# High and low part of each split stationary operand interleaved element by element in one tile

## The chip, the cores and the metric

The kernel runs on one core of a Trainium2 chip. The metric is the device time of one execution in microseconds (us). The core has a matrix engine (TensorE, rows `PE` for its matmuls and `PEld` for its loads of the stationary operand), a vector engine (VectorE, `DVE`), a scalar engine (ScalarE, `ACT`), a general engine (GpSimd, `POOL`) and a synchronising engine (`SP`) from which nearly all transfers are issued. On-chip memory has 128 partitions; a tile of shape 128x512 has 512 elements in each of them.

## What is computed

A Mamba2 layer whose output is gated by a feed-forward network with 4-bit weights, on two sequences of 512 tokens with 512 features. The reference, cut to what matters here:

```
xn   = layernorm(x)                                   # x: [2, 512, 512]
proj = xn @ in_proj_w.T                               # 8192 gate, 8192 x, 1024 B, 1024 C, 128 dt
gate, xBC, dt = split(proj)
xBC  = silu(depthwise_conv4(xBC) + conv_b)
y    = ssd(x, B, C, D, dt)                            # 128 heads of 64, 8 groups, chunks of 128 tokens
yg   = y * silu(gate)
out  = yg * rsqrt(mean(yg**2 over a group) + 1e-5) * norm_w
s    = out @ out_proj_w.T
h    = silu(xn @ W1.T) * (xn @ W3.T)                  # W1, W3: [1376, 512], unpacked from 4 bits
g    = silu(h @ W2.T)                                 # W2: [512, 1376]
return x + s * g
```

## The kernel before, in words

Projections are computed in fp32r, a 32-bit type that TensorE takes in one pass. To keep the precision of float32, each operand `a` is split into a high part `a_hi` (the value as a copy into fp32r leaves it) and a low part `a_lo = a - a_hi`, and each product is three matmuls: hi by hi, hi by lo, lo by hi. `split_mm` (lines 132 to 138) does that for the input projections: its lines 135, 136 and 137 take the stationary operand from `a_hi`, `a_hi` and `a_lo`; `out_mm` (lines 632 to 634) does it for the output projection with `y_hi`, `y_hi`, `y_lo` stationary, and line 832 for the last product of the feed-forward network with `h_hi`, `h_hi`, `h_lo` stationary. Every one of these matmuls has its own load of the stationary operand, 128 (at one place 96) columns out of 128 partitions (96 in the last of the row tiles of `h`). The moving operand has 512 columns, in line 832's last token tile twice 256. The other matmuls of the loop are in full float32, with operands that the change leaves alone, and 128 columns wide: line 544 (`fp32_chunks`), line 586 (`y_diag`), line 694 (transposes of `xt`).

The work is 16 bodies (2 sequences x 8 groups of heads) of 8 steps, each step one tile of 128 channels, software-pipelined by hand: in a step TensorE does `y_off` (L544, 3 chunks in 6 passes), `conv` (12 matmuls of `split_mm` for the tile three steps ahead), `y_diag` (L586 and L544), `gate_mm` (12 of `split_mm`, two ahead), `out_mm` (12, two behind) and `turn_x` (L694); twice in a body `project_bc` adds 12 more. The order on each engine is the order of the code; engines meet at semaphores alone.

Stationary tiles: `conv_hi[i]`, `conv_lo[i]` (lines 185 and 186: three of each, shape [4, 128], for the x, B and C projections), `gate_hi[h]`, `gate_lo[h]` (193, 194: two of each, [4, 512]), `y_hi`, `y_lo` (231, 232: [2, 512]), `up_hi`, `up_lo` (243, 244: four of each, [4, 128]), `h_hi`, `h_lo` (248, 249: [11, 1024]). The high part is written by ScalarE (lines 845, 863, 870, 977, 1135, 1166; the first six gate pieces by GpSimd, line 1495), the low part by GpSimd, which reads the source and the high part (lines 1485, 1490, 1497, 1505, 1528, 1535, 1542, 1585, 1607). In each of them the elements of a partition lie side by side, 4 bytes apart. The moving operands (`xn_hi`, `xn_lo`, `wout_hi`, `wout_lo`, `w2_hi`, `w2_lo`) are split in the same way and stay as they are.

A low part is made well ahead of its use. The semaphores `wlo_x`, `wlo_b`, `wlo_g` and `lo_done` tell TensorE that the low part of conv, B/C, gate and y tiles is there. GpSimd's step runs: `yt + ec` (1519), `yt * gate` (1523), the low parts of the weights (1528, 1535, 1542, 1546), the sum of squares (1555), the low part of y (1505).

Before the loop, tiles of a start phase (`pre`, lines 203 to 221) lie where `wout`, `acc`, `y` and others lie later; the feed-forward tiles (from line 241) lie where the loop's tiles lay.

Of the kernel before, what the change touches and what calls it, by code (L numbers as in the profile page):

```python
# [22 lines left out]
R32 = mybir.dt.float32r  # L23
I32 = mybir.dt.int32

P = 128
SEQS, SEQ, DIM = 2, 512, 512
KT = DIM // P
# [4 lines left out]
HALF = GCH // 2  # L33
# [12 lines left out]
MT = HIDDEN // P  # L46
# [104 lines left out]
def build(nc, x, w_conv, w_gate, w_out, w_dt, conv_p, norm_p, head_p, consts, w1q, w1s, w3q, w3s,  # L151
# [9 lines left out]
    with ExitStack() as ctx:  # L161
# [3 lines left out]
        def alloc(stack, name, shape, dt=F32):  # L165
            return stack.enter_context(nc.sbuf_tensor(name, [P] + shape, dt))
# [8 lines left out]
        dc_all = alloc(ctx, "dc_all", [GROUPS, TILES])  # L175
        cw_all = alloc(ctx, "cw_all", [GROUPS, CONVS, 5])
        alloc(ctx, "to_line", [40])
        ident = alloc(ctx, "ident", [P])
        mask = alloc(ctx, "mask", [P])
        xn_hi = alloc(ctx, "xn_hi", [KT, SEQS * SEQ], R32)  # L180
# [1 line left out]

        main = ExitStack()

        conv_hi = [alloc(main, f"conv_hi{i}", [KT, P], R32) for i in range(3)]
        conv_lo = [alloc(main, f"conv_lo{i}", [KT, P], R32) for i in range(3)]
        raw_x = alloc(main, "raw_x", [2, DIM])
        raw_b = alloc(main, "raw_b", [DIM])
        raw_g = alloc(main, "raw_g", [DIM])
        raw_o = alloc(main, "raw_o", [DIM])  # L190
        z = alloc(main, "z", [3, SEQ])
        b_t = alloc(main, "b_t", [SEQ])
        gate_hi = [alloc(main, f"gate_hi{h}", [KT, HALF], R32) for h in range(2)]
        gate_lo = [alloc(main, f"gate_lo{h}", [KT, HALF], R32) for h in range(2)]
        c_t = alloc(main, "c_t", [2, SEQ])
        xt = alloc(main, "xt", [4, SEQ])
        gm = alloc(main, "gm", [NC, CHUNK])
# [5 lines left out]
        pre = ExitStack()  # L203
# [7 lines left out]
        ecs = alloc(pre, "ecs", [TT, CHUNK])  # L211
        soft = alloc(pre, "soft", [TT, CHUNK])
        wdt_lo = alloc(pre, "wdt_lo", [KT, P], R32)
        heads = alloc(pre, "heads", [3])
        d_row = alloc(pre, "d_row", [P])
        pick = alloc(pre, "pick", [2, P // 2])
# [11 lines left out]
                acc = alloc(main, "acc", [TT, DIM])  # L228
        sq = alloc(main, "sq", [SEQ])
        sq_sum = alloc(main, "sq_sum", [SEQ])  # L230
        y_hi = alloc(main, "y_hi", [2, SEQ], R32)
        y_lo = alloc(main, "y_lo", [2, SEQ], R32)
        yt = alloc(main, "yt", [2, SEQ])
        ec = [alloc(main, f"ec{i}", [(NC - 1) * CHUNK]) for i in range(2)]
        xdt = alloc(main, "xdt", [NC * P])
# [4 lines left out]

        q_raw = [[alloc(ctx, f"q_raw{i}{k}", [DIM], I32) for k in range(Q_BUFS[i])] for i in range(3)]
        q_s = [[alloc(ctx, f"q_s{i}{k}", [DIM]) for k in range(Q_BUFS[i])] for i in range(3)]
        up_hi = [[alloc(ctx, f"up_hi{i}{k}", [KT, P], R32) for k in range(2)] for i in range(2)]
        up_lo = [[alloc(ctx, f"up_lo{i}{k}", [KT, P], R32) for k in range(2)] for i in range(2)]

        w2_hi = alloc(ctx, "w2_hi", [MT + 1, DIM], R32)
        w2_lo = alloc(ctx, "w2_lo", [MT + 1, DIM], R32)
        h_hi = alloc(ctx, "h_hi", [MT + 1, SEQS * SEQ], R32)
        h_lo = alloc(ctx, "h_lo", [MT + 1, SEQS * SEQ], R32)
        fa = alloc(ctx, "fa", [2, DIM])  # L250
        fh = alloc(ctx, "fh", [2, DIM])

# [1465 lines left out]
```

How the kernel before makes its waits and increments, by code:

```python
def wait(eng, sem, count):  # L84
    if isinstance(count, int) and count <= 0:
        return
    eng.wait_ge(sem, count)
# [254 lines left out]
        def token_steps(eng, b):  # L343
            eng.wait_ge(pa, (N_SOFT + N_EXPS) * b + N_SOFT)
            eng.wait_ge(pd, N_PD * b + 1)
            eng.tensor_tensor(qt[Q_DT][:, half[b], :], qt[Q_DT][:, half[b], :], ecs[:, half[b], :],
                              ALU.add).then_inc(dt_done, 1)
            eng.wait_ge(dt_done, 3 * b + 1)
            eng.tensor_scalar(qt[Q_DT][:, half[b], :], qt[Q_DT][:, half[b], :], DT_MIN, DT_MAX, ALU.max,
                              ALU.min).then_inc(dt_done, 1)
            eng.wait_ge(dt_done, 3 * b + 2)
            eng.tensor_scalar(qt[Q_CD][:, half[b], :], qt[Q_DT][:, half[b], :], heads[:, 2:3], None,
                              ALU.mult).then_inc(dt_done, 1)
# [10 lines left out]
        def wait_gate_piece(eng, group, pos):  # L365
            if group == 0 and pos < 4:
                eng.wait_ge(gate0_in[pos], 16)
            else:
                eng.wait_ge(rawg_in, 16 * (8 * group + pos - 3))
# [9 lines left out]
        def wait_hp(eng, body):  # L379
            if body.n == 0:
                eng.wait_ge(hp0_ev, NQ)
            else:
                eng.wait_ge(hp_in[body.seq], 16 * (body.group + body.seq))
# [1 line left out]
        def store_out(sp, t):  # L386
            sp.wait_ge(r2_done, t + 1)
            h = col_parts(t)[0]
            sp.dma_start(out_t[t][:, h], fh[:, t % 2, h]).then_inc(o_out[t % 2], 16)
```

## Time and profile before

| what | us |
|---|---|
| median of 3 runs | 1780.93 (1780.87 to 1780.94) |
| the profiled execution, its own time | 1780.88 |
| its span, first to last instruction | 1779.1 |
| TensorE matmuls busy | 1764.8 (99%) |
| VectorE busy | 1427.7 (80%) |
| GpSimd busy | 1261.9 (71%) |
| ScalarE busy | 1227.7 (69%) |

The span is cut into rows: a group of instructions is a line of the kernel, an engine, an operation and a shape, with its number, busy time and mean duration. Matmuls are pipelined, so the recorded duration of one (389 ns for 512 columns) is longer than the distance from its start to the start of the next; what a matmul costs in a dense stretch is read from the starts. The granted clock of TensorE was 0.999 of 2.4 GHz over the span.

### The profile page before, as it was taken

What the parts mean: (1) busy time and instruction counts of PE and PEld (TensorE: products, weight loads), DVE (VectorE), ACT (ScalarE), POOL (GpSimd) and SP (SyncE); (2) the same over time, 40 slices, a digit from 0 to 9 for tenths busy, and PEclk for the clock granted to TensorE, in tenths of its full rate; (3) what the DMA queues carried; (4) which work ended last, traced back from release to release, by engine and by line L of the source; (5) the groups of instructions that cost most, each with busy time, mean ns of one, the idle gap of its engine ahead of it and who ended that gap; (6) DMA issues with size and microseconds to landing.
All of it is one profiled execution on the core that took longest, in us unless ns stands there. A gap on an engine that the chain in (4) does not pass through costs nothing.

```text
span 1779.1 us, 30329 instructions
## 1 busy us (share of the span) xinstructions
PE 1764.8 (99%) x10357; PEld 1462.5 (82%) x10357; DVE 1427.7 (80%) x2196; ACT 1227.7 (69%) x2456; POOL 1261.9 (71%) x877
## 2 busy tenths in 40 slices
PE   8999999999999999999999999999999999999999
PEld 7788888888888888888888888888888888888877
DVE  7978878888788788788788887887887888878941
ACT  6986777777776777777867777677777677643320
POOL 5677787777777787677776787778776877676630
PEclk9999999999999999999999999999999999999999
DMA  5533343333333243333333333333333332235522
GB/s 197 165 124 101 100 131 108 94 122 107 117 107 111 97 134 96 101 111 119 117 105 98 117 124 96 116 101 115 122 90 112 109 127 96 78 109 166 150 77 95
DMA packets 122595, 202.84 MB, mean 114 GB/s; under 512 B 23056, under 2 KB 60560, under 8 KB 122192
## 3 DMA queue, kind: packets, MB, share of 16 engines
q1 hardware_dynamic: 120720, 197.32, 35.4%
q10 hardware_dynamic: 1728, 3.65, 0.5%
q8 instruction: 82, 1.34, 0.3%
q14 instruction: 65, 0.53, 0.1%
HBM read 193.57 MB, written 7.34 MB: 113 GB/s over the span
## 4 chain that ended last, share of the span: by engine, by line
PE 96%; DVE 2%; POOL 1%; issue 1%; DMA 0%; ACT 0%; SPq 0%; POOLq 0%; DVEq 0%
PE bank L135 17%; PE bank L137 17%; PE bank L136 16%; PE bank L544 11%; PE bank L586 7%; PE bank L632 6%; PE bank L634 6%; PE bank L633 6%; PE bank L832 3%; PE bank L694 3%; PE bank L675 1%; DVE z L1190 0%; PE bank L655 0%; DVE x_in L1342 0%; POOL yt L1523 0%
## 5 line engine op out<-in xcount | busy, mean ns | idle before, releaser
L1519 POOL TENSOR_TENSOR yt<-yt,ec 128x384 f32<-128x384 f32 x128 | 174.7, 1365 | 320.4 <-DVE ec L1254 320.4
L1190 DVE SCALAR_TENSOR_TENSOR z<-bank,cw_all,z 128x511 f32<-128x511 f32 (+2 forms) x477 | 356.2, 747 | 11.7 <-ACT z L945 0.4
L906 ACT ACTIVATE lm<-lm,hp 128x128 f32<-128x128 f32 x1024 | 313.2, 390 | 0.8
L135 PE MATMUL bank<-xn_hi,conv_hi 128*128 128x512 f32 x640 | 261.1, 408 | 3.5 <-DVE z L1190 3.5
L1224 DVE SCALAR_TENSOR_TENSOR lm<-lm,gm 128x1024 f32<-128x1024 f32 x128 | 261.0, 2039 | 3.5 <-ACT lm L906 3.5
L1245 DVE TENSOR_TENSOR xdt<-bank,hp 128x512 f32<-128x512 f32 x128 | 88.3, 690 | 212.8 <-PE bank L694 212.7
L137 PE MATMUL bank<-xn_hi,conv_lo 128*128 128x512 f32 x640 | 251.0, 392 | 0.0
L136 PE MATMUL bank<-xn_lo,conv_hi 128*128 128x512 f32 x640 | 250.7, 392 | 0.0
L1523 POOL TENSOR_TENSOR yt<-yt,gate 128x512 f32<-128x512 f32 x128 | 226.7, 1771 | 19.0 <-POOL yt L1519 0.9
L1528 POOL TENSOR_TENSOR conv_lo<-raw_x,conv_hi 128x512 fp32r<-128x512 f32 x124 | 218.9, 1766 | 9.8 <-ACT conv_hi L845 9.7
L135 PE MATMUL bank<-xn_hi,gate_hi 128*128 128x512 f32 x512 | 212.4, 415 | 0.0
L945 ACT ACTIVATE z<-bank,cw_all 128x512 f32<-128x512 f32 x128 | 99.1, 774 | 161.7 <-PE bank L137 161.5
L137 PE MATMUL bank<-xn_hi,gate_lo 128*128 128x512 f32 x512 | 201.4, 393 | 0.0
L632 PE MATMUL bank<-wout_hi,y_hi 128*128 128x512 f32 x512 | 199.7, 390 | 0.0
L634 PE MATMUL bank<-wout_hi,y_lo 128*128 128x512 f32 x512 | 199.5, 390 | 0.0
L633 PE MATMUL bank<-wout_lo,y_hi 128*128 128x512 f32 x512 | 199.2, 389 | 0.0
L136 PE MATMUL bank<-xn_lo,gate_hi 128*128 128x512 f32 x512 | 199.1, 389 | 0.0
L1211 DVE SCALAR_TENSOR_TENSOR lm<-hp,lm 128x1024 f32<-128x1024 f32 x128 | 194.5, 1520 | 0.0
L1505 POOL TENSOR_TENSOR y_lo<-yt,y_hi 128x512 fp32r<-128x512 f32 x128 | 182.2, 1423 | 3.0 <-ACT y_hi L977 3.0
L1555 POOL TENSOR_TENSOR sq_sum<-sq_sum,sq 128x512 f32<-128x512 f32 x111 | 145.2, 1308 | 21.3 <-ACT sq L985 21.3
L586 PEld LDWEIGHTS bank<-lm,xdt 128*64 128x64 f32 x2048 | 109.2, 136 | 45.8 <-issue 44.6
L137 PEld LDWEIGHTS bank<-xn_hi,conv_lo 128*128 128x128 f32 x640 | 120.5, 188 | 26.0
(145 smaller groups left out, 3950.3 us busy)
## 6 DMA issues: line engine op xcount, KB each, us to landing
lm<-cs_d SPq DMA_DIRECT2D x128, 512.0 KB, 4.1
raw_x<-w_conv_dram SPq DMA_DIRECT2D x128, 256.0 KB, 3.1
ec<-e_d SPq DMA_DIRECT2D x256, 96.0 KB, 3.7
raw_o<-w_out_dram SPq DMA_DIRECT2D x64, 256.0 KB, 2.7
raw_g<-w_gate_dram SPq DMA_DIRECT2D x61, 256.0 KB, 2.8
raw_b<-w_conv_dram SPq DMA_DIRECT2D x32, 256.0 KB, 3.9
q_raw<-w1q_dram SPq DMA_DIRECT2D x10, 256.0 KB, 3.6
q_s<-w1s_dram SPq DMA_DIRECT2D x10, 256.0 KB, 3.9
```

The source lines that it names most:

```text
L135: pe.matmul(dst, a_hi, b_hi, start=(i == 0), stop=False)
L136: pe.matmul(dst, a_hi, b_lo, start=False, stop=False)
L137: mm = pe.matmul(dst, a_lo, b_hi, start=False, stop=(i == len(terms) - 1))
L586: mm = pe.matmul(ps_y[HD * j:HD * j + HD, c * P:(c + 1) * P], xdt[:, c * P + HD * j:c * P + HD * j + HD], lm[n % 3][:, NC * j + c, :], sta ...
L632: pe.matmul(ps_o[c][:, :], y_hi[:, ko % 2, o], w[0], start=first, stop=False)
L633: pe.matmul(ps_o[c][:, :], y_hi[:, ko % 2, o], w[1], start=False, stop=False)
L634: mm = pe.matmul(ps_o[c][:, :], y_lo[:, ko % 2, o], w[0], start=False, stop=last)
L906: e = act.activation(lm[m % 3][:, u, :], lm[m % 3][:, u, :], ACT.Exp, bias=hp[bd.seq][:, Q_CS, k1, u:u + 1])
L1190: dve.scalar_tensor_tensor(dst[:, d:SEQ], src[:, 0:SEQ - d], cw_all[:, bd.group, pos, 3 - d:4 - d], dst[:, d:SEQ], ALU.mult, ALU.add).then ...
L1224: dve.scalar_tensor_tensor(lm_c, lm_c, 1.0, gm[:, :, :].rearrange("p c l -> p (c l)").unsqueeze(1) .broadcast_to((P, 2, SEQ)), ALU.mult, A ...
L1523: pool.tensor_tensor(yt[:, kp % 2, :], yt[:, kp % 2, :], gate[:, kp % 4, :], ALU.mult).then_inc(yg_done, 1)
L1528: pool.tensor_tensor(conv_lo[kx % 2][:, :, :], raw_x[:, kx % 2, :].rearrange("p (k j) -> p k j", k=KT), conv_hi[kx % 2][:, :, :].bitcast(F ...
```

## The change

The high and the low part of each of the five kinds of stationary tile become one tile with a last dimension of 2. The high part is every even element, the low part every odd one. All writes, reads and loads of these parts now have a step of 8 bytes in place of 4. Nothing else is edited: the same instructions stand on each engine in the same order with the same waits, and a load of the stationary operand has `[2, 128]` (step 2 elements, 128 of them) in place of `[1, 128]`. Together the pair takes the bytes that its two tiles took. `past_y` is a tile that nobody uses: it moves the small start tiles behind the last byte of the new `y_w`. The moving operands stay contiguous.

```diff
+        def alloc_pair(stack, name, shape):
+            t = alloc(stack, name, shape + [2], R32)
+            return t[:, :, :, 0], t[:, :, :, 1]
...
-        conv_hi = [alloc(main, f"conv_hi{i}", [KT, P], R32) for i in range(3)]
-        conv_lo = [alloc(main, f"conv_lo{i}", [KT, P], R32) for i in range(3)]
+        conv_hi, conv_lo = zip(*[alloc_pair(main, f"conv_w{i}", [KT, P]) for i in range(3)])
...
-        gate_hi = [alloc(main, f"gate_hi{h}", [KT, HALF], R32) for h in range(2)]
-        gate_lo = [alloc(main, f"gate_lo{h}", [KT, HALF], R32) for h in range(2)]
+        gate_hi, gate_lo = zip(*[alloc_pair(main, f"gate_w{h}", [KT, HALF]) for h in range(2)])
...
+        alloc(pre, "past_y", [DIM])
...
-        y_hi = alloc(main, "y_hi", [2, SEQ], R32)
-        y_lo = alloc(main, "y_lo", [2, SEQ], R32)
+        y_hi, y_lo = alloc_pair(main, "y_w", [2, SEQ])
...
-        up_hi = [[alloc(ctx, f"up_hi{i}{k}", [KT, P], R32) for k in range(2)] for i in range(2)]
-        up_lo = [[alloc(ctx, f"up_lo{i}{k}", [KT, P], R32) for k in range(2)] for i in range(2)]
+        up_hi, up_lo = zip(*[zip(*[alloc_pair(ctx, f"up_w{i}{k}", [KT, P]) for k in range(2)]) for i in range(2)])
...
-        h_hi = alloc(ctx, "h_hi", [MT + 1, SEQS * SEQ], R32)
-        h_lo = alloc(ctx, "h_lo", [MT + 1, SEQS * SEQ], R32)
+        h_hi, h_lo = alloc_pair(ctx, "h_w", [MT + 1, SEQS * SEQ])
```

## Rows read from the trace of the kernel before

**Rows 1.** The page: the span and the busy time of each engine.
```profile
span 1779.1 us, 30329 instructions
PE 1764.8 (99%) x10357; PEld 1462.5 (82%) x10357; DVE 1427.7 (80%) x2196; ACT 1227.7 (69%) x2456; POOL 1261.9 (71%) x877
```
**Rows 2.** The page, part 4: the chain that ended last, by engine.
```profile
PE 96%; DVE 2%; POOL 1%; issue 1%; DMA 0%; ACT 0%; SPq 0%; POOLq 0%; DVEq 0%
```
**Rows 3.** Matmuls in time (start us, us, line, out<-in, count), one step.
```profile
802.12 0.60 PE L694 MATMUL bank<-ident,xt 128*128 128x128 f32 x4
802.55 0.83 PE L544 MATMUL bank<-c_t,state 128*128 128x128 f32 x6
803.14 0.48 PE L135 MATMUL bank<-xn_hi,conv_hi 128*128 128x512 f32 x1
803.46 0.39 PE L136 MATMUL bank<-xn_lo,conv_hi 128*128 128x512 f32 x1
...
810.63 0.39 PE L632 MATMUL bank<-wout_hi,y_hi 128*128 128x512 f32 x1
```
**Rows 4.** Loads of the stationary operand in time, same place.
```profile
802.45 0.75 PEld L544 LDWEIGHTS bank<-c_t,state 128*128 128x128 f32 x6
803.12 0.19 PEld L135 LDWEIGHTS bank<-xn_hi,conv_hi 128*128 128x128 f32 x1
803.23 0.19 PEld L136 LDWEIGHTS bank<-xn_lo,conv_hi 128*128 128x128 f32 x1
```
**Rows 5.** Matmuls in time: the last of one `out_mm`, and the next step's.
```profile
813.12 0.39 PE L634 MATMUL bank<-wout_hi,y_lo 128*128 128x512 f32 x1
...
815.26 0.48 PE L135 MATMUL bank<-xn_hi,conv_hi 128*128 128x512 f32 x1
...
822.74 0.39 PE L632 MATMUL bank<-wout_hi,y_hi 128*128 128x512 f32 x1
...
825.23 0.39 PE L634 MATMUL bank<-wout_hi,y_lo 128*128 128x512 f32 x1
```
**Rows 6.** Matmuls by form: full float32, and a moving operand of 256 columns.
```profile
L544 PE MATMUL bank<-xw,b_tok 128*128 128x128 f32 x768 | 119.7, 292 | 0.0
L544 PE MATMUL bank<-c_t,state 128*128 128x128 f32 x768 | 107.9, 277 | 0.0
L832 PE MATMUL bank<-w_lo,h_hi 128*128 128x256 f32 x20 | 5.7, 283 | 0.0
```
**Rows 7.** Matmuls in time, moving operand of 256 columns.
```profile
1769.15 0.28 PE L832 MATMUL bank<-w_hi,h_lo 128*128 128x256 f32 x1
...
1770.35 0.28 PE L832 MATMUL bank<-w_hi,h_hi 128*128 128x256 f32 x1
```
**Rows 8.** Groups by form: writes of 512 elements, contiguous and with a step.
```profile
L1177 ACT ACTIVATE fh<-bank 128x512 f32<-128x512 f32 x7 | 4.2, 597 | 46.8 <-PE bank L832 46.8
L1040 ACT ACTIVATE stage<-bank 128x512 f32<-128x512 f32 x4 | 4.1, 1141 | 0.5 <-PE bank L752 0.5
L1261 DVE COPY b_tok<-bank 128x512 f32<-128x512 f32 x16 | 10.9, 681 | 0.0
L1370 DVE COPY stage<-bank 128x512 f32<-128x512 f32 x4 | 4.1, 1094 | 0.5 <-PE bank L752 0.5
L1391 DVE COPY pick<-ident 128x64 f32<-128x64 f32 x2 | 0.3, 179 | 0.0
L1389 DVE COPY d_row<-heads 128x128 f32<-128x128 f32 x1 | 0.2, 156 | 0.0
```
**Rows 9.** What GpSimd waited for: us in total, times, longest.
```profile
POOL yt L1519 <- DVE ec L1254: 320.4, 123, 4.6
```
**Rows 10.** GpSimd in time, one step.
```profile
808.56 1.30 POOL L1528 TENSOR_TENSOR conv_lo<-raw_x,conv_hi 128x512 fp32r<-128x512 f32 x1
...
812.83 1.28 POOL L1505 TENSOR_TENSOR y_lo<-yt,y_hi 128x512 fp32r<-128x512 f32 x1
```
**Rows 11.** What VectorE waited for: us in total, times, longest.
```profile
DVE xdt L1245 <- PE bank L694: 212.7, 77, 4.0
```

## The prediction

> **What bounds the kernel now.** I read the page first, for the busy times; then the chain that ended last; then the timeline of TensorE and of its loads over one step, since a duration of a pipelined matmul does not tell its cost; then the groups of instructions by form, for anything that already moves data with a step; last the waits of GpSimd and VectorE. TensorE's matmuls are busy for 1764.8 of 1779.1 us, the next engine for 1427.7 [rows 1], and 96% of the chain that ended last is TensorE's [rows 2]. So there is one bound from end to end. The change can matter in two ways: a load of the stationary operand comes to set the pace of matmuls, or a writer (ScalarE, GpSimd) becomes so slow that TensorE waits.
>
> What one matmul costs: from 822.74 to 825.23 us there are 11 distances between the starts of 12 matmuls of 512 columns, 0.226 us each; the same from 810.63 to 813.12 [rows 3, 5]. What one load costs when nothing covers it: six loads start at 802.45 and the next at 803.12, 0.112 us each [rows 4]. A load for the next matmul starts as the matmul before it starts, so in a dense stretch of 512 columns it may take up to 0.226 us before it is seen: 2.02 times its present time, or 0.114 us more. That slack decides this case.
>
> **The change part by part.** Number, order and waits of the instructions stay, and no transfer touches the changed tiles. Three things get another price.
>
> *First, the loads.* The changed ones, counted from the code: 160 projections by conv and B/C, 128 by gate, 128 of the output, 44 of the feed-forward network's first half, each with 12 loads, and 231 in its second half with 512 columns moving: 5751 in all, each behind a slack of 0.114 us. 66 more (11 row tiles x 3 terms x 2 halves) have 256 columns moving and start 0.120 us apart, ten distances from 1769.15 to 1770.35 [rows 7]: their slack is 0.008 us. And some have none: where `conv` and `gate_mm` follow the 128-column float32 matmuls, loads set the pace. In rows 3 and 4 conv's first load starts at 803.12, its second at 803.23, and the second matmul at 803.46; 803.46 minus one matmul of 0.226 is 803.23, just when the first load of 0.112 is over. So the first load of `conv` and of `gate_mm` is on the path in full. Each of the two forms of line 544 has 768 rows, 6 to a step [rows 6], so there are 128 such places for each, 256 in all.
>
> No row shows a load with a step. The trace does have writes whose elements lie 16 bytes apart (`stage`, where the step is one chunk count of 4 elements): ScalarE takes 1141 ns for 512 of them against 597 contiguous, VectorE 1094 against 681 [rows 8]. That is 1.06 and 0.81 ns more for an element, 0.136 and 0.103 us more for a load of 128. The two ends lie on both sides of the slack. By VectorE's price a load takes 0.215 us, hidden behind 512 columns; seen are 256 x 0.103 = 26.4 and 66 x (0.215 - 0.120) = 6.3, together +32.7 us. By ScalarE's it takes 0.248: 5751 x 0.022 = 126.5, 256 x 0.136 = 34.8 and 66 x 0.128 = 8.4, together +170 us. The other end is zero. It isn't below zero by much: a dense matmul doesn't wait for its load, so a cheaper one gives nothing back there.
>
> I take zero. The step is 8 bytes, not 16, and what TensorE already reads is the nearest thing to it: the moving operand streams 512 x 4 = 2048 bytes of each partition in 0.226 us, 9.1 bytes per ns [rows 3, 5], and a load with the new step passes over 1024 bytes in 0.112 us, also 9.1 bytes per ns. Memory that feeds the one rate to one operand of this engine should feed it to the other. The only access with a step of 8 bytes in the trace, VectorE's read of `ident` into `pick`, is unclear: 64 elements take 179 ns where 128 of a broadcast value take 156 [rows 8]. Either the step costs something or the broadcast runs in a faster form; it doesn't exclude a small price.
>
> The rows with 16 bytes cost nearly double for ScalarE. The Trainium skill (Advanced Engine Details and Errata, SBUF Cachelines) says why that might be: lines are 16 bytes, accesses that stay in a line run at full rate, and two hits in a line are needed to hide the memory's latency. A step of 16 bytes gives one hit, one of 8 bytes gives exactly two. By that rule the sum is +0, by the 16-byte rows it is +33 to +170 us. The trace agrees with the half of the rule that it shows; no run here yet shows the half about 8 bytes.
>
> *Second, the high parts.* 390 writes by ScalarE and 6 by GpSimd. At most 0.544 us more each [rows 8], 212 us in all; that takes ScalarE from 1227.7 to 1440 us busy of 1779, about where VectorE stands. I take zero by the same argument: 512 elements in 597 ns, 1.17 ns each, is a slower walk than the loads'. What hides it otherwise: ScalarE's idle time, 31% of the span [rows 1].
>
> *Third, the low parts.* 396 instructions of GpSimd now read the high part and write the low part with the step. 3.1 of them fall to a step. What hides a longer one is GpSimd's wait for VectorE's product `ec`, 320.4 us in 123 places, 2.6 us a step [rows 9]; so each may grow by about 0.84 us before GpSimd's own step grows. With ScalarE's 16-byte price charged once, 0.54 us, that holds. The deadlines are looser still: a conv low part ends at 809.86 and its first load comes near 815.24, 5.4 us later; a y low part ends at 814.11 and its matmuls begin at 822.74, 8.6 us later [rows 3, 5, 10]. Once that cover is gone, `yt` comes late, then y's low part, then `out_mm`. I take zero. GpSimd also shares time with VectorE, which has 212.7 us of waiting for TensorE to lose [rows 11].
>
> The Trainium skill (GPSIMD Engine Reference, section 7, performance pitfalls for Q7 kernels) gives reads with a step over 8 bytes half as much time again; 8 bytes is on its free side. By an estimate from it, were 8 bytes charged after all, a low part of 1.29 us would take some 0.65 us more, and the sum would still be +0, under the 0.84 us of cover.
>
> **The sum.** 1780.88 + 0 + 0 + 0 = 1780.9 us. The profiled execution took 1780.88 us, its span 1779.1; the median of the runs is 1780.93, so no correction is needed. A measurement of this kernel tells some 0.2%, 3.6 us, from no change.
>
> **The rivals.**
>
> *A, the forecast: no price at 8 bytes.* For it: the equal 9.1 bytes per ns, and 0.114 us of cover over some 5500 of the 5817 loads. Its own range is 1778.5 to 1783. Chance 0.67.
>
> *B, slower: a load costs more but stays inside the slack.* One mechanism, in one kind of place: loads where nothing streams long enough to cover them. It decides from a load that is 0.013 us longer (256 x 0.013 is 3.3 us, and 66 times the 0.005 over the slack is 0.3). Half of VectorE's 16-byte price, 0.052 us: 256 x 0.052 + 66 x 0.044 = +16, 1797 us. All of it: 1814 us. For it: `pick`; and both 16-byte rows, which show that steps are not free as such. Against: the step is half of theirs. Chance 0.14.
>
> *C, slower by much: a load passes 2.02 times its time.* Then every dense matmul is paced by its load; 1780.9 + 170 = 1951 us at ScalarE's price. For it: that row. Against: it needs more than a doubling at half the step. Chance 0.05.
>
> *D, slower by the writers.* If the low parts pay ScalarE's 16-byte price for the read and for the write, 1.09 us, a GpSimd step grows by 3.4 us against 2.6 of cover; 0.8 x 128 is +102, 1883 us. With one of the two it is hidden, and VectorE's waits for GpSimd's turns leave some 5 us. Chance 0.07.
>
> *E, faster.* Both parts now lie in the same lines. If that made a load cheaper, only the 256 + 66 uncovered ones would show it; at half of 0.112 us that is 256 x 0.056 and, down to the 256 columns' own time, almost nothing for the 66: -14, 1767 us. Nothing in the trace speaks for it, except that the first loads are on the path. Chance 0.07.
>
> That the step is not there is excluded: the program's loads carry it.
>
> **How the numbers follow.** The predicted time is A's. The range must leave out at most 0.2: C (0.05), most of E (0.05) and the upper part of D (0.05) are left out, B is inside up to VectorE's price. That gives 1777 to 1815. Faster is E, 0.07; the same is A, 0.67; slower is B, C and D, 0.26.
>
> **What would show it.** In the changed kernel's profile the loads of conv, gate, y, up and h should still last 188 ns, and be as many; the starts of `out_mm`'s matmuls should be 0.226 us apart, those of 256 columns 0.120, and conv's second matmul 0.32 us behind its first. ScalarE's high parts should last 0.62 us and GpSimd's undisturbed low parts 1.29. B would show as loads of over 200 ns with `out_mm` unmoved at 0.226 and the 256-column matmuls spread; C as `out_mm` itself spread; D as low parts over 2.1 us and TensorE waiting for GpSimd or VectorE. A longer or shorter load in the dense stretch with the total unmoved would make my price wrong and my sum right. The prediction is wrong if the time leaves 1777.3 to 1784.5.

## The result: 26.2 us slower, and the profile after

| | before | after |
|---|---|---|
| median of the runs | 1780.93 us | 1807.16 us (1806.95 to 1808.15) |
| ratio | | 1.0148 [1.0131, 1.0166] |
| profiled execution, its span | 1780.9, 1779.1 us | 1807.1, 1805.3 us |
| granted clock of TensorE | 0.999 | 0.999 |

I had forecast no change. The time lies inside the range that I gave, but the kernel is 26.2 us slower, seven times the 3.6 us that I had taken for the limit of what a measurement tells from no change. From line 544 on, the lines of after stand one further down than those of before (L544 is L545).

The page of after, parts 1 and 4 (beside [rows 1, 2]):
```profile
span 1805.3 us, 30329 instructions
PE 1791.7 (99%) x10357; PEld 1496.4 (83%) x10357; DVE 1432.9 (79%) x2196; ACT 1240.6 (69%) x2456; POOL 1269.9 (70%) x877
PE 97%; DVE 2%; issue 0%; DMA 0%; POOL 0%; SPq 0%; ACT 0%; DVEq 0%
```
The span grew by 26.2 us and TensorE's busy time by 26.9, with the same 10357 matmuls. Its part of the chain is 97%, before 96%. So the time is within TensorE's work, and not in a wait for someone else.

Matmuls of after in time, one step (beside [rows 3, 5]):
```profile
801.91 0.83 PE L545 MATMUL bank<-c_t,state 128*128 128x128 f32 x6
802.50 0.48 PE L135 MATMUL bank<-xn_hi,conv_w 128*128 128x512 f32 x1
802.82 0.39 PE L136 MATMUL bank<-xn_lo,conv_w 128*128 128x512 f32 x1
803.04 0.39 PE L137 MATMUL bank<-xn_hi,conv_w 128*128 128x512 f32 x1
...
810.06 0.39 PE L633 MATMUL bank<-wout_hi,y_w 128*128 128x512 f32 x1
810.29 0.39 PE L634 MATMUL bank<-wout_lo,y_w 128*128 128x512 f32 x1
...
812.63 0.39 PE L635 MATMUL bank<-wout_hi,y_w 128*128 128x512 f32 x1
```
Here lies most of the difference. From 810.06 to 812.63 us the 12 matmuls of one `out_mm` start 0.2336 us apart; before it was 0.226. The durations beside them, 0.39 us, are those of before and show nothing: the ends are modelled, the starts aren't.

Loads of after in time, the same place (beside [rows 4]):
```profile
801.91 0.64 PEld L545 LDWEIGHTS bank<-c_t,state 128*128 128x128 f32 x5
802.47 0.20 PEld L135 LDWEIGHTS bank<-xn_hi,conv_w 128*128 128x128 f32 x1
802.59 0.20 PEld L136 LDWEIGHTS bank<-xn_lo,conv_w 128*128 128x128 f32 x1
802.82 0.19 PEld L137 LDWEIGHTS bank<-xn_hi,conv_w 128*128 128x128 f32 x1
803.05 0.19 PEld L135 LDWEIGHTS bank<-xn_hi,conv_w 128*128 128x128 f32 x1
```
The uncovered first load lasts from 802.47 to 802.59, 0.120 us where it took 0.112. From then on each load starts with a matmul, 0.23 us after the load before it. It has far more time than it needs, and the matmuls spread all the same.

Matmuls of after with a moving operand of 256 columns, in time (beside [rows 7]):
```profile
1794.88 0.29 PE L833 MATMUL bank<-w_lo,h_w 128*128 128x256 f32 x1
1795.00 0.40 PE L833 MATMUL bank<-w_hi,h_w 128*128 128x256 f32 x2
...
1797.16 0.41 PE L833 MATMUL bank<-w_hi,h_w 128*128 128x256 f32 x2
```
From 1795.00 to 1797.16 lie 18 matmuls, counting each x2 as two: 0.120 us apart as before.

Groups by form of after: writers and loads (beside [rows 8, 10]):
```profile
L1529 POOL TENSOR_TENSOR conv_w<-raw_x,conv_w 128x512 fp32r<-128x512 f32 x124 | 221.3, 1784 | 10.0 <-ACT conv_w L846 10.0
L1506 POOL TENSOR_TENSOR y_w<-yt,y_w 128x512 fp32r<-128x512 f32 x128 | 185.0, 1445 | 3.1 <-ACT y_w L978 3.1
L136 PEld LDWEIGHTS bank<-xn_lo,conv_w 128*128 128x128 f32 x640 | 124.5, 195 | 20.1
L978 ACT ACTIVATE y_w<-yt 128x512 fp32r<-128x512 f32 x128 | 86.2, 673 | 60.8 <-POOL yt L1524 60.8
L846 ACT ACTIVATE conv_w<-raw_x 128x512 fp32r<-128x512 f32 x128 | 84.8, 663 | 0.0
L1486 POOL TENSOR_TENSOR conv_w<-raw_x,conv_w 128x512 fp32r<-128x512 f32 x4 | 5.2, 1312 | 1.8 <-ACT conv_w L846 1.8
```
The writers pay little. ScalarE's high part of `conv` took 617 ns before and takes 663, that of y 624 and 673. GpSimd's undisturbed low part of `conv` went from 1292 to 1312, that of y from 1423 to 1445. In all ScalarE is busy 12.9 us longer, GpSimd 8.0.

Waits of after (beside [rows 9, 11]):
```profile
POOL yt L1520 <- DVE ec L1255: 333.3, 123, 4.7
DVE xdt L1246 <- PE bank L695: 226.8, 80, 4.4
```
Both grew, by 12.9 and 14.1 us. The engines beside TensorE wait longer for it; that is what a slower TensorE looks like from their side.

**Where the 26.2 us lie.** For each kind of matmul I took the mean distance between the starts of neighbours of that kind in the whole trace, leaving out those over 0.3 us (a first, uncovered load, or a wait). Those of conv, gate and output are counted apart, in the last row:

| | places | before, ns | after, ns | sum, us |
|---|---|---|---|---|
| conv and B/C | 1627 | 228.5 | 233.0 | 7.3 |
| gate | 1281 | 230.7 | 232.7 | 2.6 |
| output | 1404 | 226.8 | 233.3 | 9.1 |
| feed-forward, first half (`up`), loads of 128 columns | 470 | 226.9 | 233.3 | 3.0 |
| second half (`h`), 512 columns | 230 | 227.3 | 233.5 | 1.4 |
| second half, 256 columns | 65 | 119.7 | 119.9 | 0.0 |
| behind a first, uncovered load | 267 | 313 | 319 (medians) | 1.6 |

The rows give 25.0 us. 122 places where `out_mm` follows `gate_mm` at once (226.7 ns before, 233.9 after) and 30 where conv follows the output (226.7 and 233.4) add 1.1. Of 26.2 us 0.1 is left. Only 1.6 us lie where my rival B had put the price.

### The profile page after: what moved, and what is told of

The parts are those of the page before. It is cut to its first block, busy times and chain, and to the rows that moved or that the text cites. A ratio compares the mean times of both kernels' runs of the same rounds, so it can differ in the third digit from the quotient of the medians.

```text
span 1805.3 us, 30329 instructions
## 1 busy us (share of the span) xinstructions
PE 1791.7 (99%) x10357; PEld 1496.4 (83%) x10357; DVE 1432.9 (79%) x2196; ACT 1240.6 (69%) x2456; POOL 1269.9 (70%) x877
## 4 chain that ended last, share of the span: by engine, by line
PE 97%; DVE 2%; issue 0%; DMA 0%; POOL 0%; SPq 0%; ACT 0%; DVEq 0%
PE bank L135 17%; PE bank L136 17%; PE bank L137 17%; PE bank L545 12%; PE bank L587 7%; PE bank L633 7%; PE bank L634 7%; PE bank L635 7%; PE bank L833 3%; PE bank L695 3%; PE bank L676 1%; DVE z L1191 0%; PE bank L656 0%; DVE x_in L1343 0%; DMA x_in<-x_dram 0%
## 5 line engine op out<-in xcount | busy, mean ns | idle before, releaser
L1246 DVE TENSOR_TENSOR xdt<-bank,hp 128x512 f32<-128x512 f32 x128 | 88.3, 690 | 228.4 <-PE bank L695 226.8
L135 PE MATMUL bank<-xn_hi,conv_w 128*128 128x512 f32 x640 | 264.4, 413 | 3.3 <-DVE z L1191 3.3
L137 PE MATMUL bank<-xn_hi,conv_w 128*128 128x512 f32 x640 | 252.8, 395 | 0.0
L136 PE MATMUL bank<-xn_lo,conv_w 128*128 128x512 f32 x640 | 252.8, 395 | 0.0
L1524 POOL TENSOR_TENSOR yt<-yt,gate 128x512 f32<-128x512 f32 x128 | 226.7, 1771 | 19.0 <-POOL yt L1520 0.9
L1529 POOL TENSOR_TENSOR conv_w<-raw_x,conv_w 128x512 fp32r<-128x512 f32 x124 | 221.3, 1784 | 10.0 <-ACT conv_w L846 10.0
L135 PE MATMUL bank<-xn_hi,gate_w 128*128 128x512 f32 x512 | 213.1, 416 | 0.0
L633 PE MATMUL bank<-wout_hi,y_w 128*128 128x512 f32 x512 | 202.3, 395 | 0.0
L634 PE MATMUL bank<-wout_lo,y_w 128*128 128x512 f32 x512 | 201.8, 394 | 0.0
L635 PE MATMUL bank<-wout_hi,y_w 128*128 128x512 f32 x512 | 201.8, 394 | 0.0
L137 PE MATMUL bank<-xn_hi,gate_w 128*128 128x512 f32 x512 | 201.6, 394 | 0.0
L136 PE MATMUL bank<-xn_lo,gate_w 128*128 128x512 f32 x512 | 201.6, 394 | 0.0
L1506 POOL TENSOR_TENSOR y_w<-yt,y_w 128x512 fp32r<-128x512 f32 x128 | 185.0, 1445 | 3.1 <-ACT y_w L978 3.1
L137 PEld LDWEIGHTS bank<-xn_hi,conv_w 128*128 128x128 f32 x640 | 124.3, 194 | 25.4
```

The source lines that it names most:

```text
L135: pe.matmul(dst, a_hi, b_hi, start=(i == 0), stop=False)
L136: pe.matmul(dst, a_hi, b_lo, start=False, stop=False)
L137: mm = pe.matmul(dst, a_lo, b_hi, start=False, stop=(i == len(terms) - 1))
L633: pe.matmul(ps_o[c][:, :], y_hi[:, ko % 2, o], w[0], start=first, stop=False)
L634: pe.matmul(ps_o[c][:, :], y_hi[:, ko % 2, o], w[1], start=False, stop=False)
L635: mm = pe.matmul(ps_o[c][:, :], y_lo[:, ko % 2, o], w[0], start=False, stop=last)
```

## The experiments

The theories at the start were: the loads cost more; the writers do; it is the place of the tiles. Unless said otherwise a kernel is the one of before with the edit shown, and its ratio is to that kernel on the same chip. Where loads take elements other than their own, the sums come out of permuted or mixed stationary operands, while the number, sizes and order of the instructions stay.

### Loads alone, writers alone

`e1_loads8` keeps the two separate tiles and lets only the loads step over 8 bytes, so that they read a mixture of neighbouring blocks.
```diff
+def stepped(flat, i, s, n=128):
+    first, last = (128 * s * (i // s), 128 * s * (i // s + 1)) if s != 3 else ((0, 384) if i < 3 else (128, 512))
+    return flat[:, first:last].rearrange("p (m j) -> p j m", j=s)[:, i % s, 0:n]
...
-                    (conv_hi[2][:, q, :], conv_lo[2][:, q, :], xn_hi[:, q, t], xn_lo[:, q, t])
+                    (stepped(joined(conv_hi[2]), q, 2), stepped(joined(conv_lo[2]), q, 2), xn_hi[:, q, t], xn_lo[:, q, t])
```
(and so for gate, y, up and h; `joined` joins the two free dimensions.)

> The kernel before, with its contiguous tiles and contiguous writes; only TensorE's loads of conv, gate, y, up and h take 128 elements with a step of 8 bytes out of the same tile, so that channels or tokens are permuted and the output is not the reference's. Theory L (the loads alone cost, some 6.7 ns for each dense matmul): about 1807 us, out_mm's starts 0.233 us apart, load rows of 193 to 195 ns. Theory W (the writers with a step make it slower, by contention for memory with TensorE): 1781 us, starts 0.227 apart. Theory T (high and low part in one tile, same lines loaded twice in a row): 1781 us too.

`e2_writers8` is the changed kernel, whose writers step over 8 bytes into the interleaved tiles, but whose loads read 128 elements that lie together, halves of both parts mixed.
```diff
+def packed(row, i, n=128):
+    flat = row.rearrange("p k j -> p (k j)")
+    return flat[:, 256 * i:256 * i + n], flat[:, 256 * i + 128:256 * i + 128 + n]
...
-                        pe.matmul(ps_o[c][:, :], y_hi[:, ko % 2, o], w[0], start=first, stop=False)
+                        pe.matmul(ps_o[c][:, :], packed(whole["y_w"][:, ko % 2, :, :], c)[0], w[0], start=first, stop=False)
```

> The changed kernel's tiles, written and read by ScalarE and GpSimd with the step of 8 bytes, but TensorE loads 128 contiguous elements of them, high and low mixed, so the output is not the reference's. Theory L: 1781 us (at most 1783), starts of out_mm 0.227 us apart, high parts of ScalarE at 0.66 us as in the changed kernel. Theory W: about 1807 us. Theory T: about 1807 us.

Measured: e1 1806.5 us, 1.0146 [1.0129, 1.0163]; e2 1781.06, 1.0002 [0.9992, 1.0012]. The loads alone make 25.8 us; the writers' +0.4 can't be told from zero. In e1 the distances are those of after to 0.1 ns, with ScalarE and GpSimd as fast as before:
```profile
PE 1789.7 (99%) x10357; PEld 1494.6 (83%) x10357; DVE 1429.1 (79%) x2196; ACT 1227.8 (68%) x2456; POOL 1262.3 (70%) x877
```

### Covered or uncovered loads: y alone

The y tiles alone are interleaved; what is computed stays. Every load of `out_mm` runs beside a matmul of 512 columns, so by my slack argument this had to be free.
```diff
+        alloc(pre, "past_y", [DIM])
...
-        y_hi = alloc(main, "y_hi", [2, SEQ], R32)
-        y_lo = alloc(main, "y_lo", [2, SEQ], R32)
+        y_w = alloc(main, "y_w", [2, SEQ, 2], R32)
+        y_hi, y_lo = y_w[:, :, :, 0], y_w[:, :, :, 1]
```

> Only the y tile is interleaved, 128 x 12 = 1536 dense matmuls. Theory L with a fee per dense matmul: 1536 x 6.67 ns = 10.2 us, so 1791 us, out_mm's starts 0.233 apart, conv's and gate's as before (0.227 to 0.236). Rival B of the prediction (only uncovered loads cost): y's loads are all covered, so 1781 us.

Measured: 1791.35 us, 1.0059 [1.0042, 1.0076]. The first and the last matmul of one `out_mm` of e3:
```profile
816.09 0.39 PE L633 MATMUL bank<-wout_hi,y_w 128*128 128x512 f32 x1
...
818.65 0.40 PE L635 MATMUL bank<-wout_hi,y_w 128*128 128x512 f32 x1
```
These are 11 distances of 0.233 us (233.3 ns in the mean of all). Gate stays at 230.7 ns, and conv goes from 228.5 to 229.4. 1536 loads x 6.5 ns are 10.0 us, and +10.7 were found. So a load that is hidden, and ends long before it is wanted, slows the matmul that hides it.

### Larger steps

The same edit with steps of 16 bytes (`s` = 4) and 12 bytes (`s` = 3):

> As the first, with a step of 16 bytes in all five kinds of load (output permuted, not the reference's). Lines theory (the fee grows with the 16-byte lines that a load touches, 32, 64, 128, by 0.208 ns a line): 20 ns more than contiguous for a dense matmul, starts 0.247 us apart, some 1880 to 1896 us. Flat fee (any step costs the same): 1807 us, 0.233 apart. Rate theory (at one element a line the load runs at ScalarE's 16-byte price, 0.248 us): starts 0.25 or more apart, 1910 to 1951 us.

> All five kinds of load with a step of 12 bytes (output permuted, not the reference's). The 16-byte run showed uncovered loads 0.213 us apart (1.67 ns an element) against 0.112 contiguous and 0.120 with 8 bytes. Line theory (the load's port delivers one 16-byte line in 1.67 ns): 0.75 of a line an element, 1.25 ns, uncovered loads about 0.160 us apart, load rows about 188 + 53 = 241 ns, the 66 matmuls of 256 columns about 0.17 apart; dense ones stay covered with the fee of 7 to 8 ns; total 1781 + 38 - 12 + 249 x 0.05 + 66 x 0.05, about 1822 to 1826 us. Cliff theory (everything below 16 bytes is free, but for a flat fee): 1807 us, load rows of 194 ns. Halving theory (any step over 8 bytes costs as much as 16): 1854 us, load rows of 310 ns.

Measured: e4 1854.48 us, 1.0413 [1.0396, 1.0431]; e5 1836.0, 1.0314 [1.0296, 1.0331]. Groups of loads by form, e4 and then e5:
```profile
L144 PEld LDWEIGHTS bank<-xn_hi,conv_hi 128*128 128x128 f32 x640 | 198.1, 310 | 3.7 <-DVE z L1199 2.2 <-POOL conv_lo L1537 1.1
```
```profile
L144 PEld LDWEIGHTS bank<-xn_hi,conv_hi 128*128 128x128 f32 x640 | 161.5, 252 | 2.5 <-DVE z L1199 1.1 <-POOL conv_lo L1537 1.1 <-issue 0.2
```
e4 in time, loads, then matmuls, where conv begins:
```profile
806.61 0.31 PEld L144 LDWEIGHTS bank<-xn_hi,conv_hi 128*128 128x128 f32 x1
806.82 0.34 PEld L145 LDWEIGHTS bank<-xn_lo,conv_hi 128*128 128x128 f32 x1
807.08 0.31 PEld L146 LDWEIGHTS bank<-xn_hi,conv_lo 128*128 128x128 f32 x1
```
```profile
806.64 0.60 PE L144 MATMUL bank<-xn_hi,conv_hi 128*128 128x512 f32 x1
807.08 0.40 PE L145 MATMUL bank<-xn_lo,conv_hi 128*128 128x512 f32 x1
807.32 0.40 PE L146 MATMUL bank<-xn_hi,conv_lo 128*128 128x512 f32 x1
```
The uncovered load takes 806.82 - 806.61 = 0.21 us (0.213 in most places), and 0.166 with 12 bytes. At 16 bytes it is 1.67 ns an element. Now the uncovered places show a price, as I had worked it for such a step: at 267 places the distance behind the first load grows by 0.127 us, 33.9 us in all (0.101 of it is the longer load, the rest the slower first matmul), and 66 x (0.2316 - 0.1197) = 7.4. Dense stretches reach 234 to 236 ns, another 33. The sum is 74, and +73.8 were measured. For 12 bytes the same terms give 17.0 + 3.5 + 36 = 56, against +55.7.

Two things follow. A load almost twice as long (0.213 against 0.120) adds only 1.3 ns to the dense distance of `out_mm`, so that distance isn't paced by the load's length. And the loads of these runs fit about 1.67 ns for each 16 bytes of memory that they touch: 128 such pieces take 0.213 us, and the 96 that a 12-byte step touches would take 0.160, where 0.166 was found. 64 pieces at 8 bytes would be 0.107; it is 0.120. (The price of a piece is an estimate from these three times.)

### A step of 32 bytes, gate alone
```diff
-                        (gate_hi[kg // 4][:, q, o], gate_lo[kg // 4][:, q, o], xn_hi[:, q, t], xn_lo[:, q, t])
+                        (stepped(joined(gate_hi[kg // 4]), q * 4 + kg % 4, 8), stepped(joined(gate_lo[kg // 4]), q * 4 + kg % 4, 8), xn_hi[:, q, t], xn_lo[:, q, t])
```

> Only gate's 1536 loads, with a step of 32 bytes (output permuted, not the reference's). Line theory: 32 bytes touch one line an element as 16 do, so what the 16-byte run showed for gate: load rows of 312 ns, the first load 0.127 us longer at 128 places, dense starts 0.235 apart instead of 0.231: 16.3 + 5.9, together about 1803 us. Theory that the load slows on with the step (as with wider lines or banks): load rows over 400 ns and dense gate starts at 0.3 us or more, 1880 us or above.

Measured: 1820.07 us, 1.0224 [1.0207, 1.0241], between the two expectations. The loads' rows last 329 ns against 310 at 16 bytes, an uncovered one takes 0.218 us, and the matmuls beside them start 243.8 ns apart. Over gate that is 1281 x 13.1 ns = 16.8 us, and 127 first loads x 0.135 us = 17.1. Another 1404 x 3.5 ns = 4.9 come in `out_mm`, whose own loads were left alone. These last I had not expected; where they come from is read from the traces at the end of this section.

### The moving operand with a step

The loads are contiguous; `up` takes every second of 1024 columns of xn as its moving operand.
```diff
-                    (up_hi[i][k][:, kk, 0:rows], up_lo[i][k][:, kk, 0:rows], xn_hi[:, kk, t], xn_lo[:, kk, t])
+                    (up_hi[i][k][:, kk, 0:rows], up_lo[i][k][:, kk, 0:rows],
+                 *(v[:, kk, :].rearrange("p (m j) -> p j m", j=2)[:, b, :] for v in (xn_hi, xn_lo)))
```

> Loads as before; the moving operand of the 528 matmuls of up, and of these alone, has a step of 8 bytes (it takes every second token of both sequences, output not the reference's). Line theory (a port delivers one 16-byte line in 1.67 ns, which the contiguous moving operand already needs in full: 4 elements at 0.417 ns): two elements a line, so 512 columns take 0.427 us, starts about 0.44 apart, 528 x 0.213 = +112 us less what the end of the loop hides, 1880 to 1895 us. Argument of the prediction (memory feeds 9.1 bytes a ns): the same doubling. Theory that 8 bytes are free for TensorE's ports as such (two hits in a line): 1781 to 1785 us.

Measured: 1901.7 us, 1.0678 [1.066, 1.0695]. The same step that costs a load 0.008 us doubles a moving stream: `up` goes from 226.9 to 451 ns, 528 x 0.224 = 118 of the 121 us. Groups of `up` by form, e8 and then before:
```profile
L136 PE MATMUL bank<-xn_lo,up_hi 128*128 128x512 f32 x160 | 101.2, 632 | 0.0
```
```profile
L136 PE MATMUL bank<-xn_lo,up_hi 128*128 128x512 f32 x160 | 62.3, 389 | 0.0
```
By the estimate above, 512 elements with this step touch 256 pieces of 16 bytes, at 1.67 ns 0.427 us; a contiguous stream touches 128 in 0.213, which is also what 512 columns need at 2.4 GHz. By it the contiguous float32 stream has no room left: it already asks for a piece every 1.67 ns. That is a reading of one run, which measured the doubling and not the pieces.

### The same contiguous loads, begun elsewhere

If the cause is two streams that clash, and not the load's own length, then contiguous loads that merely begin at another address should show it. Each load of 128 elements begins `s` elements later (the last block of a row earlier), so it reads a shifted block.
```diff
+def stepped(flat, i, s, n=128):
+    first = 128 * i + s if i < 3 else 384 - s
+    return flat[:, first:first + n]
```

> Contiguous loads that begin 4 bytes off a line (output not the reference's): 33 lines instead of 32 for each. Theory that the fee comes from a load that needs one line in every 1.67 ns: a contiguous load has half of that need, so no fee, 1781 us, out_mm's starts 0.227 apart. Theory that any load but an aligned contiguous one pays (a fast form is lost): 1807 us, 0.233 apart, load rows of 194 ns.

The next four were meant to shift by 8, 16, 32 and 64 bytes. By an error of mine in writing them all four begin 4 bytes off, so they are repeats of e7, and their expectations were not put to the test by them:

> Contiguous loads that begin 8 bytes off a 16-byte line (output not the reference's). The 4-byte shift cost as much as the step of 8 bytes in dense stretches (0.2327 us between starts against 0.2268) while its load rows stayed at 188 ns, so the fee is no longer load. Theory P (the fee is a clash between the load's and the moving operand's walk through memory, and a contiguous load that begins on a line escapes part of it): a shift of 8 bytes pays too, 1798 to 1806 us, starts 0.231 to 0.235. Theory E (only a start on an odd element pays): 1781 us.

> Contiguous loads that begin on a 16-byte line, but one line off their 64 bytes (output not the reference's). Theory P with 16-byte lines: no fee, 1781 us, starts 0.227. Theory P with groups of 64 bytes or with four banks by line (the relative place of load and moving operand counts): it moves, either way, to between 1765 and 1806 us.

> As before with 32 bytes. 16-byte lines: 1781 us. Groups of 64 bytes or banks: moved from 1781, and differently from the 16-byte shift.

> As before with 64 bytes. 16-byte lines, and groups of 64 bytes: 1781 us, starts 0.227. Wider groups (the tiles now all begin on a multiple of 512 bytes, 256 or 128): moved from 1781.

Measured: e7 1802.39 us, 1.0124 [1.0107, 1.014]; the four others 1802.62, 1802.21, 1802.37 and 1802.51, which tells how well such a price repeats. Then the shifts proper, `s` = 2, 4, 16 and 64:

> Contiguous loads that really begin 8 bytes off a 16-byte line (the four runs before, meant for 8 to 64 bytes, all began 4 bytes off by my error and repeat the 4-byte run; output not the reference's). Theory P16 (a start off a 16-byte line pays): about 1802 us, out_mm's starts 0.2327 us apart. Theory P8 (a start off 8 bytes pays): 1781 us, 0.2268.

> Contiguous loads that begin on a 16-byte line, 16 bytes off a 64-byte group (output not the reference's). P16: no fee, 1781 us, starts 0.2268 apart. Wider groups, or banks by line so that the relative place to the moving operand counts: moved, between 1765 and 1806 us.

> Contiguous loads that begin 64 bytes off (output not the reference's). P16, and groups of 64 bytes: 1781 us, starts 0.2268. Moved from 1781 only if groups wider than 64 bytes count.

> Contiguous loads that begin 256 bytes off their tile's place (output not the reference's). If the pattern repeats within 256 bytes: 1781 us, starts 0.2268. If it is wider: about 1790 to 1806 us.

And all tiles together 64 bytes further, nothing else changed and what is computed the same:
```diff
-        alloc(ctx, "to_line", [40])
+        alloc(ctx, "to_line", [56])
```

> The kernel before with every tile from ident on moved by 64 bytes, loads and moving operands together (to_line has 56 elements instead of 40). Clash theory (relative place of load and moving operand counts): 1781 us, starts 0.2268 apart. Absolute theory (a load must begin on a multiple of 512 or so): 1805 us, 0.233.

| loads begin | us | ratio | conv | gate | output | up (128 columns) | h (512) |
|---|---|---|---|---|---|---|---|
| as before | 1780.93 | | 228.5 | 230.7 | 226.8 | 226.9 | 227.3 |
| 4 bytes off | 1802.39 | 1.0124 | 231.8 | 232.5 | 232.7 | 232.8 | 232.6 |
| 8 | 1797.74 | 1.0096 [1.0079, 1.0113] | 231.3 | 231.2 | 231.4 | 232.1 | 231.3 |
| 16 | 1789.08 | 1.0048 [1.0031, 1.0065] | 227.9 | 232.2 | 231.0 | 227.3 | 232.8 |
| 64 | 1805.26 | 1.014 [1.0123, 1.0157] | 233.3 | 232.6 | 233.0 | 232.8 | 233.0 |
| 256 | 1780.55 | 0.9998 [0.9988, 1.0008] | as before | | | | |
| every tile 64 | 1780.93 | 1.0 [0.9991, 1.001] | as before | | | | |

(The five columns on the right are mean distances of dense matmuls in ns.) Contiguous loads, no longer than before, make most of the loss once they begin elsewhere, and with 64 bytes nearly all of it. Loads of `out_mm` by form, then the first and the last matmul of one `out_mm`, e7:
```profile
L641 PEld LDWEIGHTS bank<-wout_hi,y_hi 128*128 128x128 f32 x512 | 96.0, 188 | 22.7
```
```profile
808.10 0.39 PE L641 MATMUL bank<-wout_hi,y_hi 128*128 128x512 f32 x1
...
810.66 0.39 PE L643 MATMUL bank<-wout_hi,y_lo 128*128 128x512 f32 x1
```
Moving the loads alone by 64 bytes costs 25 us; moving all tiles by 64 costs nothing. So what counts is where the load lies relative to other accesses, and by the shift of 256 bytes the pattern has come round again. No place tried gives a faster kernel than the one before.

### The moving operand stands still

The last run takes the clash away from its other side. In conv, B/C and gate the moving operand is one column, repeated 512 times with a step of zero; conv's loads are contiguous, gate's step over 8 bytes. `up` and the output are left as before (the expectation below counts `up` in, but the edit doesn't touch it).
```diff
-                        (gate_hi[kg // 4][:, q, o], gate_lo[kg // 4][:, q, o], xn_hi[:, q, t], xn_lo[:, q, t])
+                        (stepped(gate_hi[kg // 4][:, q, :], kg % 4, 2), stepped(gate_lo[kg // 4][:, q, :], kg % 4, 2), *(v[:, q, t.start:t.start + 1].broadcast_to((P, SEQ)) for v in (xn_hi, xn_lo)))
```

> The moving operand of conv, gate and up is one column, read 512 times (step 0), so that it walks through no memory; conv's loads stay contiguous, gate's have the step of 8 bytes; the output projection is as before (output not the reference's). Clash theory: with nothing to clash with, conv and gate have the same distance between starts, at or below 0.2268 us (down to 0.213 to 0.216, 512 columns at 2.4 GHz), the whole at or below 1781 us, by 3488 x 0.012 = 42 us at most. Theory that the load itself holds up the array: conv 0.227 to 0.229, gate 0.233 as with the step before, 1784 to 1790 us.

Measured: 1743.2 us, 0.9786 [0.977, 0.9803]. e18 in time, gate:
```profile
812.34 0.47 PE L144 MATMUL bank<-xn_hi,gate_hi 128*128 128x512 f32 x1
812.64 0.38 PE L145 MATMUL bank<-xn_lo,gate_hi 128*128 128x512 f32 x1
812.86 0.38 PE L146 MATMUL bank<-xn_hi,gate_lo 128*128 128x512 f32 x1
813.08 0.38 PE L144 MATMUL bank<-xn_hi,gate_hi 128*128 128x512 f32 x1
...
814.37 0.38 PE L144 MATMUL bank<-xn_hi,gate_hi 128*128 128x512 f32 x1
```
From 812.64 to 814.37 are 8 distances of 0.216 us, and conv, with contiguous loads, has 0.216 as well. The loads themselves stay as they were with either step, conv and then gate:
```profile
L145 PEld LDWEIGHTS bank<-xn_lo,conv_hi 128*128 128x128 f32 x640 | 121.7, 190 | 14.3
L145 PEld LDWEIGHTS bank<-xn_lo,gate_hi 128*128 128x128 f32 x512 | 100.2, 196 | 8.0
```
So a stepped load is some 6 ns longer by itself, wherever it is; and the dense matmul pays for the step only while its moving operand walks through memory. With the moving operand still, both kinds of load give the same distance. 216 ns is 2.7 over what 512 columns take at 2.4 GHz. The kernel before pays 11 to 15 ns more than that, after 17. How much of the 11 is the load's is not shown: in no run does the moving operand walk through memory with no load beside it.

**The output's 230.3 ns in e6 and e18.** In both runs the output's loads and moving operand are those of before, and yet its mean distance is 230.3 ns, where before has 226.8. The traces say where the 3.5 ns lie. Medians of the distance from each matmul of a group of 12 to the next, in ns:

| from matmul | 1 | 2 | 3 | 4 | 5 | 6 | 7 | 8 | 9 | 10 | 11 | 12 |
|---|---|---|---|---|---|---|---|---|---|---|---|---|
| before, gate | 313 | 229 | 233 | 236 | 224 | 231 | 236 | 228 | 232 | 231 | 227 | 227 |
| before, conv | 314 | 231 | 235 | 228 | 232 | 231 | 227 | 227 | 227 | 227 | 227 | |
| before, output | 227 | 227 | 227 | 227 | 227 | 227 | 227 | 227 | 227 | 227 | 227 | |
| e6, output | 229 | 233 | 236 | 224 | 231 | 236 | 228 | 232 | 231 | 227 | 227 | |
| e18, output | 232 | 233 | 236 | 224 | 231 | 236 | 228 | 232 | 231 | 227 | 227 | |

In e6 in time, the first five matmuls of one output:
```profile
817.43 0.39 PE L641 MATMUL bank<-wout_hi,y_hi 128*128 128x512 f32 x1
817.66 0.40 PE L642 MATMUL bank<-wout_lo,y_hi 128*128 128x512 f32 x1
817.89 0.40 PE L643 MATMUL bank<-wout_hi,y_lo 128*128 128x512 f32 x1
818.13 0.39 PE L641 MATMUL bank<-wout_hi,y_hi 128*128 128x512 f32 x1
818.36 0.39 PE L642 MATMUL bank<-wout_lo,y_hi 128*128 128x512 f32 x1
```
Before, gate begins behind an uncovered load, runs through a fixed series of nine distances, and has settled at 227 ns when the output takes over. In e6 and e18 gate runs at another distance, and the output goes through the same series at its own start. In gate of before and in the output of e6 some 95 of 100 places or more lie within 1 ns of these medians, at every position. A wait or another engine's accesses would hardly repeat so exactly. So in these runs the distance of two matmuls goes with where their loads lie and also with how many matmuls of the same stretch went before them. The same holds in the kernel before: gate (230.7) and conv (228.5) lie above the output (226.8) by the distances at their start, and end at the same 227.

## Why the prediction was wrong

- **The bound** [rows 1, 2] was read rightly: TensorE from end to end, before and after.
- **The step that failed** is the one the case hung on: "in a dense stretch of 512 columns it may take up to 0.226 us before it is seen", and, following from it, `out_mm` "unmoved at 0.226". It asks only when a load ends. A load that ends in time still slows the matmul that covers it. e3 shows it (10.7 us, nearly all of it in covered loads), e7 shows it with loads not a nanosecond longer, and e18 shows that the price of the step goes when the moving operand no longer walks through memory. That the two take turns at something in memory is my reading of these three; what they share is not shown. I gave this term +0 for some 5500 loads; it measured 24 of the 26 us.
- **The equal rates.** "Memory that feeds the one rate to one operand of this engine should feed it to the other" took a coincidence for spare capacity. e8 suggests that 9.1 bytes per ns was near the moving stream's limit (the double stretch of memory takes twice the time). What two such streams do to each other when they run at the same time is a thing the comparison didn't cover. The row of before held a hint: at a granted clock of 0.999 of 2.4 GHz, 512 columns need 0.213 us, and I read 0.226 without asking what the other 13 ns were. e18 took 11 of them back.
- **The load's own price**: forecast 0, measured 0.008 us where it is uncovered. It is under the 0.013 from which rival B decides. The distance behind the first load grows by 6 ns at 267 places, 1.6 us; but it grows by the same 6 ns in e7, whose first load still takes 0.112 us, so even this part can't be put down to the load's length. The 256-column matmuls at 0.120, conv's second matmul at 0.32 and the number of loads came as said. The loads' rows went to 194 ns, where I had said 188.
- **The writers**: right. ScalarE's high parts take 0.045 us more where the 16-byte bound allowed 0.544, GpSimd's low parts 0.02, and e2 puts both together at +0.4 us, with zero inside its interval. The covers named for them (ScalarE's idle time, GpSimd's wait for `ec`) held.
- **The rivals.** 1807 lies within B's prices (1781 to 1814), but by accident: B put them in the uncovered loads alone. The spread of `out_mm` was the sign that I had named for C, but C needs a load of over 0.226 us, and the loads' rows went from 188 to 194 ns. The chance of slower by all paths, 0.26, was too low, since I had no rival in which a covered load costs anything before it ends too late. e4 shows B's own mechanism when it is there: 41 us at 16 bytes, with an uncovered load of 0.213 us where VectorE's row had given 0.215. B by VectorE's price had 33 us, since the first matmul behind the load, slower too, was not in its sum.
- **The rule about lines.** A load that touches each line of 16 bytes twice is nearly as fast as a contiguous one (0.120 against 0.112), and one that touches it once is not (0.213). The Trainium skill (Advanced Engine Details and Errata, SBUF Cachelines) has full rate at two hits in a line; by that rule the sum was +0, and the runs say: nearly so for the load, not so for the matmul beside it, and not at all for a moving operand, which doubles (e8).
- **The engine's two read streams.** With the moving operand still, matmuls are 216 ns apart; with a walking one 227 to 231 beside the contiguous loads of before, 233 beside stepped ones. The Trainium skill (TensorE: Matmul & The Clock Gate, step ① LDWEIGHTS) says the opposite, that loading weights takes no read bandwidth from the matmul under way. Here the measurement decides.

**What stays open.** Why the relative place of a load counts is not shown, only that it does, that 256 bytes is a whole number of turns of the pattern (128 was not tried), and that 64 is the worst of the shifts tried. Nor is it shown why the distances go through a series before they settle, or how much of the settled 227 ns is the load's. No kernel here with the reference's output beats the one before.

## What to carry to other kernels

Before calling an operation hidden because it ends in time, ask what it shares with the one that hides it: the price of a hidden load stands in the start-to-start distances of the matmuls beside it, not in its own row or its end. Take these distances by position in a group before you look for another engine: here a fixed series at the start of a stretch explained what looked like someone else's doing. Where a bound engine runs a few per cent over its pure column time, look into that gap first: here a change of layout (a step, or only another start address) widened it at every one of thousands of matmuls. In these runs steps of 8 bytes were cheap for the writers, cost 1.5% of the kernel in the loads, and doubled the time of a moving float32 operand.

## What the runs showed of the hardware that was not expected

- Where a covered load begins changes the distance of the matmuls beside it: 226.8 ns in the output as before, 231 to 233 with starts 4, 8, 16 or 64 bytes off, 216 in conv and gate when the moving operand reads one column only. Shifts of 256 bytes, or of all tiles together, change nothing.
- Behind a disturbed matmul the distances of contiguous loads run 229, 233, 236, 224, 231, 236, 228, 232, 231 ns and settle at 227 (gate of before, output of e6). Conv has a shorter series, 231, 235, 228, 232, 231.
- An uncovered load of 128 float32 columns: 0.112 us contiguous, 0.120 at 8 bytes, 0.166 at 12, 0.213 at 16. At 32 bytes it takes 0.218, its row is longer again (329 ns against 310), and its matmul is at 243.8.
- A moving operand of 512 float32 columns at 8 bytes takes 451 ns, twice its contiguous time.
- ScalarE's write of 512 elements at 8 bytes costs 0.045 us on 0.62, GpSimd's read and write 0.02 on 1.29; at 16 bytes ScalarE had needed 1141 ns instead of 597 [rows 8].
